# A block of gated experts, windowed attention and gated experts on one core: logits computed transposed, the gate products of the first and the last pass taken from PSUM, and a new order of the steps

## What is computed

```python
x = x + 0.5 * ffn(layernorm(x))
x = x + attn(layernorm(x))          # 16 heads, each token sees itself and the 63 before it
x = x + 0.5 * ffn(layernorm(x))     # the same weights as the first
```

```python
shared = silu(X @ sW1 + sb1) @ sW2 + sb2
logits = einsum('btd,ed->bte', X, routing_W) + expert_bias
top_vals, top_idx = top_k(sqrt(softplus(logits)), 2)
combine = sum(one_hot(top_idx, 8) * top_vals[..., None], axis=-2)
hdn = silu(einsum('nd,edh->enh', X, rW1) + rb1)
routed = einsum('ne,end->nd', combine, einsum('enh,ehd->end', hdn, rW2) + rb2)
```

## Time and profile before

| | |
|---|---|
| median of 3 runs | 1568.83 us (1565.42 to 1570.04) |
| the profiled execution | 1562.98 us, of it a span of 1561.1 us from the first to the last instruction |
| busy: PE, DVE, ACT, POOL | 97%, 76%, 72%, 51% |
| PE busy | 1506.6 us in 13969 matmul records |
| steps that mark the stages | aX0=0 at 74.95 us, O0=0 at 163.6 us, O0=1 at 259.6 us, O0=13 at 1351.3 us, S0=15 at 1428.03 us, O0=15 at 1502.93 us |

### The profile page before, as it was taken

One profiled execution on the slowest core, in us unless ns is written; L12 is line 12 of the kernel. 1 busy time (PEld: TensorE's weight loads), 2 busy tenths in 40 slices (PEclk: granted clock), 3 DMA queues, 4 the chain that ended last, 5 costly groups with the idle time before them and its releaser, 6 DMA issues.

```text
span 1561.1 us, 41431 instructions
## 1 busy us (share of the span) xinstructions
PE 1506.6 (97%) x13969; PEld 1359.6 (87%) x13969; DVE 1186.7 (76%) x4773; ACT 1127.8 (72%) x3416; POOL 790.8 (51%) x794
## 2 busy tenths in 40 slices
...
GB/s 118 15 203 103 148 120 186 106 137 133 119 170 96 188 119 131 136 125 168 104 187 112 137 130 135 157 119 177 109 138 141 119 159 108 174 108 155 84 28 14
DMA packets 264392, 199.66 MB, mean 128 GB/s; under 512 B 150859, under 2 KB 220918, under 8 KB 264182
## 3 DMA queue, kind: packets, MB, share of 16 engines
...
## 4 chain that ended last, share of the span: by engine, by line
PE 59%; DVE 15%; SPq 8%; issue 7%; ACT 5%; DMA 5%; POOL 2%; DVEq 0%; POOLq 0%; ACTq 0%
PE gb L1048 8%; PE gb L1050 8%; PE gb L1049 8%; PE yb L1048 6%; PE yb L1050 5%; PE yb L1049 5%; PE ptb L1121 4%; PE sb_ L1112 4%; SPq L570 4%; PE cxb L1140 3%; ACT pr L717 2%; SPq L565 2%; PE gb L1162 2%; DVE pr L920 1%; DVE ag L998 1%
## 5 line engine op out<-in xcount | busy, mean ns | idle before, releaser
L664 POOL TENSOR_TENSOR gl<-ag,gh 128x512 fp32r<-128x512 f32 x288 | 376.2, 1309 | 267.2 <-ACT gh L762 266.1
L647 POOL TENSOR_TENSOR pr<-pr,rinv 128x512 f32<-128x512 f32 x256 | 274.4, 1074 | 279.5 <-DVE rinv L928 276.6
L717 ACT ACTIVATE pr<-pr,mx 128x128 f32<-128x128 f32 x1024 | 396.4, 391 | 8.7 <-DVE mx L920 6.6
L1048 PE MATMUL yb<-w2h,gh 128*128 128x256 f32 x1152 | 334.7, 291 | 10.5 <-POOL gl L664 10.4
L1050 PE MATMUL yb<-w2l,gh 128*128 128x256 f32 x1152 | 321.7, 279 | 0.0
L1049 PE MATMUL yb<-w2h,gl 128*128 128x256 f32 x1152 | 321.6, 279 | 0.0
L775 ACT ACTIVATE tt<-gb,b1half 128x512 f32<-128x512 f32 x288 | 195.3, 680 | 130.1 <-PE gb L1050 125.9
L920 DVE CUSTOM_DVE_ANT_0 pr<-sb_,mask 128x128 f32<-128x128 f32 x1024 | 235.4, 285 | 36.8 <-issue 25.8
L992 DVE SCALAR_TENSOR_TENSOR ag<-gb,b,gate 128x512 f32<-128x512 f32 x256 | 190.0, 744 | 89.3 <-ACT tt L775 55.7
L1048 PE MATMUL gb<-xh,w1h 128*128 128x512 f32 x576 | 243.2, 422 | 1.7 <-DVE ag L992 1.3
L762 ACT ACTIVATE gh<-ag 128x512 fp32r<-128x512 f32 x288 | 179.9, 625 | 88.3 <-DVE ag L998 68.1
...
## 6 DMA issues: line engine op xcount, KB each, us to landing
...
ks<-qk_dram SPq DMA_DIRECT2D x256, 128.0 KB, 2.9
qs<-qk_dram SPq DMA_DIRECT2D x512, 64.0 KB, 2.5
...
```

Source lines behind the costliest of these rows:

```text
L647: nc.gpsimd.tensor_tensor(pr[:, k], pr[:, k], rinv[:, k, :].unsqueeze(2).to_broadcast([P, NP, P]), ALU.mult).then_inc(a_pn, 1)
L664: nc.gpsimd.tensor_tensor(gl[:, k, :], ag[:, k, :], gh[:, k, :].bitcast(F32), ALU.subtract).then_inc(f_gl, 1)
L717: nc.scalar.activation(pr[:, k, r, :], pr[:, k, r, :], ACT.Exp, bias=mx[:, k, r:r + 1], scale=-1.0, accum_out=rsum[:, k, r:r + 1]).then_in ...
L1048: nc.tensor.matmul(dst, ah, bh, start=start, stop=False, **kw)
```

## The change

It has five parts.

1. **Logits.** The routing weights (high and low half, padded with zeros to 128 columns) become the stationary operand, and the tokens stream past in 4 matmuls of 512 columns. A new ACT step `lt` copies the 128x512 result to the end of `xn`. A new PE step `M` multiplies each of its four 128x128 slices by a constant `fold` of 8 columns, which adds the halves and turns the logits back. `Lr` has one operation less.
2. **First and last pass.** Step `a` only adds the bias, and its result waits in a buffer that is free there (`kept`: halves of the residual buffers for experts 1 to 4, `gate` or `pt` for 5 to 8). `g` works in place. A new DVE step `m` multiplies it by the gate straight from `sb_` or `ptb` into `ag`. The eight ACT copies K of each of the two passes are gone, and with them their wait: H, t, a and g no longer need the gates.
3. **Buffers.** T of the second `ffn` writes to `axn`, and OUT reads it there. aR no longer waits for OUT; aN2 waits for the OUT of three samples before, T for the aX of two samples ahead. The last sample uses `xin` and the `p` half of `xh` and `xl`, so its start needs nothing of sample 14.
4. **Start.** Raw weights are staged in `gate`, `x2` and `axn`, and Wz waits for none of them any more. GpSimd has two more clears and two more selects.
5. **Order.** All of `HEAD`, `ORDER` and `TAIL` is new. Fillers fall from 159 to 88, all in `HEAD`.

```diff
-Z26=15 qX0=15 qX1=15 Z6=15 qL=15 qH0=15 Z30=15 qY0=15 qC=15 qH1=15 qH2=15 qH3=15 qB0=15 qB1=15 qB2=15 qB3=15
+S14=15 qY0=14 P12=15 S15=15 U11=15 P13=15 U13=15 P14=15 P15=15 qC=14 U15=15 O0=15 O1=15 qH1=14 qH2=14 qH3=14
...
-        rw = sb("rw", [P, KC, 2 * E], F32R)
+        rw = sb("rw", [P, KC, P], F32R)
+        fold = sb("fold", [P, E])
...
+        def kept(s, e):
+            if s[0] == "p" and e > 4:
+                return gate[:, e - 5, :]
+            if s[0] == "q" and e > 4:
+                return pt[:, e - 5, :]
+            two = (x1 if s[0] == "p" else [xin[(B - 2) % NXI], x1[(B - 2) % NX1]])[(e - 1) // 2]
+            u = 2 * ((e - 1) % 2)
+            return two[:, u:u + 2, :].rearrange("p t d -> p (t d)")
...
                 if s == "Wz":
                     nc.gpsimd.memset(qs[:].bitcast(F32), 0.0).then_inc(w_zero, 1)
-                    pool.wait_ge(w_lo, max(lo_done("1r"), lo_done("1t")))
                     nc.gpsimd.memset(va[:], 0.0).then_inc(w_zero, 1)
...
+                    wait(act, x_out, 16 * (b - 2))
...
+                elif s[1:] == "lt":
+                    n = nth(s, b)
+                    act.wait_ge(f_lgt, n + 1)
+                    nc.scalar.activation(lgt, bank(s[0] + "L", b), ACT.Copy).then_inc(f_lgs, 1)
...
-                elif s[1] == "K":
-                    n, m = nth(s, b), int(s[2])
-                    act.wait_ge(f_gpe, E * (s[0] == "q") + m + 1)
-                    wait(act, f_a, NE * (n - 1) + m + 6 if m < 4 else NE * n + m - 2)
-                    nc.scalar.activation(gate[:, m % 4, :], spread_to(m), ACT.Copy).then_inc(f_gk, 1)
...
-                op(nc.vector.tensor_tensor(lg[:], acc[:, :, E:2 * E], ebias[:].unsqueeze(1).to_broadcast([P, NT, E]),
-                                           ALU.add))
-                op(nc.vector.tensor_tensor(lg[:], acc[:, :, 0:E], lg[:], ALU.add))
+                op(nc.vector.tensor_tensor(lg[:], psum[:, 0:NT * E].rearrange("p (t e) -> p t e", t=NT),
+                                           ebias[:].unsqueeze(1).to_broadcast([P, NT, E]), ALU.add))
...
-                    wait(dve, x_out, 16 * b)
-                    nc.vector.tensor_tensor(x2[:, 2 * h:2 * h + 2, :],
+                    nc.vector.tensor_tensor(res(b)[:, 2 * h:2 * h + 2, :],
...
+                elif s[1] == "m":
+
+                    e = int(s[2])
+                    g = NE * nth(s, b) + e
+                    dve.wait_ge(f_gpe, E * (s[0] == "q") + e)
+                    dve.wait_ge(f_g, g + 1)
+                    wait(dve, f_gl, g + 1 - NG)
+                    nc.vector.tensor_tensor(ag[:, g % NG, :], kept(s, e), spread_to(e - 1), ALU.mult).then_inc(f_m, 1)
...
+                        rd, wr = res(b), axn
+                        dve.wait_ge(a_xt, min(2 * b + 6, 2 * B))
...
+                    for k in range(KC):
+                        nc.tensor.matmul(tile, rw[:, k, :], xh[:, q, k, :], start=(k == 0), stop=False)
+                        mm = nc.tensor.matmul(tile, rw[:, k, :], xl[:, q, k, :], start=False, stop=(k == KC - 1))
+                    mm.then_inc(f_lgt, 1)
+                elif s[1] == "M":
+                    n = nth(s, b)
+                    pe.wait_ge(f_lgs, n + 1)
                     for t in range(NT):
-                        ts = slice(t * P, (t + 1) * P)
-                        for k in range(KC):
-                            nc.tensor.matmul(tile[:, 2 * E * t:2 * E * t + 2 * E], xh[:, q, k, ts], rw[:, k, :],
-                                             start=(k == 0), stop=False, skip_group_check=True)
-                            mm = nc.tensor.matmul(tile[:, 2 * E * t:2 * E * t + E], xl[:, q, k, ts], rw[:, k, 0:E],
-                                                  start=False, stop=(k == KC - 1), skip_group_check=True)
+                        mm = nc.tensor.matmul(bank(s[0] + "L", b)[:, E * t:E * t + E], lgt[:, t * P:(t + 1) * P], fold[:],
+                                              start=True, stop=True, skip_group_check=True)
```

More of the change, by code:

```diff
@@ L21 @@
     "PE": """
[L22 to L26, removed]
+pY5-4 pH7-4 pH8-4 qH0-6 P5-5 pY6-4 S8-5 P6-5 U5-5 qC-6 S9-5 pY7-4 P7-5 S10-5 pY8-4 qH1-6 qH2-6 qY0-6 S11-5
@@ L30 @@
[L30 to L34, removed]
+qgh0-6 ph7-5 pN2-3 qt1-6 ex10-5 qt2-6 pxh0-3 cth0-5 qgh1-6 aN2-4 qgh2-6 qt3-6 qt4-6 pxh1-3 ph8-5 ex11-5
@@ L61 @@
[L61 to L69, removed]
+Z14=0 Wt=0 pX0=0 pX1=0 Z4=0 pL=0 pH0=0 pH1=0 pM=0 Z4=0 pH2=0 pH3=0 Z16=0 pY0=0 Z12=0 pC=0 pH4=0 pB0=0 pB1=0
+Z6=0 pB2=0 pB3=0 pH5=0 pH6=0 pH7=0 pY1=0 pH8=0 pY2=0 pB4=0 pB5=0 pX0=1 pY3=0 pX1=1 pY4=0 pB6=0 pB7=0 pY5=0
@@ new lines @@
+pxh0=3 aN2=2 qgh1=0 pxh1=3 qt3=0 qgh2=0 ex11=1 qt4=0 ph8=1 cth0=1 qgh3=0 axh0=2 axh1=2 qgh4=0 ph9=1 plt=3
+ex12=1 qt5=0 pen=3 qh00=2 ph10=1 qh01=2 ph11=1 qt6=0 ex13=1 qgh5=0 qt7=0 qt8=0 qgh6=0 qh10=2 ph12=1 ex14=1
+ph13=1 qgh7=0 pt0=3 ex15=1 qgh8=0 ph14=1 pcr=3 qh11=2 pct=3 pgh0=3 ph15=1 ex0=2 vh0=2 cth1=1 ex1=2 ex2=2
+vh1=2 ph0=2 ex3=2 pt1=3 pt2=3 ph1=2 qN2=1 pgh1=3 ph2=2 pt3=3 qxh0=1 pgh2=3 pt4=3 ex4=2 ph3=2 ex5=2 qxh1=1
+pgh3=3 pgh4=3 ex6=2 pt5=3 pt6=3 qlt=1 ph4=2 pgh5=3 qen=1 pgh6=3 pt7=3 pt8=3 ex7=2 ph5=2 qt0=1 pgh7=3 ph6=2
@@ new lines @@
+qH2=12 S11=13 pX0=15 qY0=12 pX1=15 P8=13 U7=13 qH3=12 S12=13 qH4=12 aX0=14 qY1=12 aX1=14 qY2=12 pL=15 P9=13
+qH5=12 pM=15 S13=13 Q00=14 P10=13 Q01=14 qY3=12 P11=13 qY4=12 P12=13 U9=13 U11=13 Q10=14 S14=13 Q11=14 pC=15
+S15=13 P13=13 qH6=12 qY5=12 P14=13 qH7=12 U13=13 P15=13 qH8=12 pH0=15 qY6=12 S0=14 U15=13 V0=14 qY7=12
+qY8=12 S1=14 P0=14 V1=14 pY0=15 pH1=15 O0=13 P1=14 O1=13 S2=14 pH2=15 pH3=15 S3=14 pY1=15 pH4=15 S4=14
+pH5=15 P2=14 qX0=13 S5=14 U1=14 P3=14 S6=14 pY2=15 qX1=13 pY3=15 pH6=15 pH7=15 qL=13 P4=14 pY4=15 qM=13
```

436 lines of the change are left out of this document (234 added, 202 removed).

## The result

The changed kernel takes 1606.66 us (median of 4 runs, 1598.16 to 1609.3) against 1567.12 us of the kernel before in the same session: ratio 1.0244, 95% interval 1.0198 to 1.029. It is slower by 2.4%; 1554 was forecast, and no rival named a cause like the one found. The profiled execution took 1607.88 us, its span 1606.2.

The account below looks back on a forecast made before the run. PE was taken to bound the kernel, busy 1506.6 of 1561.1 us, with waste at the ends. Terms -10 - 3 + 1 - 2 - 2 = -16 us, from 1568.8, gave 1554 us, range 1542 to 1571.

Parts of the forecast that it names:

- Ramp and middle: From 100 us through the middle samples: new order -2 us in the ramp, 0 in the middle, bounds -8 and +10.
- the tail: From S0=15 to the end: 58 + 65 = 123 us instead of 133.1, so -10 us, bounds -20 and -4.
- The second rival: End of kernel: attention of sample 15 stays at 70 us, partly at 1.2 GHz; no change, 1567 us; chance 0.14.
- Start: First stretch, bound by DVE: T=0 at 64.4 us, aX0=0 at 73; -2 us, bounds -5 and +3.
- the -3 of the moved V0, P14, U11 and U13: Four PE steps moved from before S0=15 to behind it; 3 us of PE work leave the full part.
- Ramp from S0 to O0=1: From 100 to 259.6 us: new order may save some idle time and half clock; -2 us, bounds -10 and +6.
- an attention of 70 us: Sample 15's attention stretch staying at 70 us instead of 58, tail 135 us, time 1567; also listed as a wrong sign.
- Logits: Each of 32 passes: four matmuls 0.92 us plus M 0.89 against 1.78 before; +1 us in all.
- The +29 us: Logits in 32 passes if each float32 pass had its own load, M costing 16 x 0.11; +29 us instead of +1.
- The first rival: Middle passes: M comes late, waiting for the ACT copy of the logits; 1 us a pass gives 1581; chance 0.12.
- What would show it: Signs: no filler behind 75 us, T=0 at about 64, tail 58 and 65 us, samples 91 us apart; also wrong signs.
- the mark of a wrong prediction: Middle samples: a round over 91.5 us, one of the listed signs that the forecast is wrong.

Follow-up runs that it names:

- the repaired kernel: Changed kernel with gates first on SP, S6 behind Y1, pN1 behind ri6, prs behind pn6, sp4 and sp5 ahead of ST10: 1551.14 us, ratio 0.9908.
- the kernel with H3 three times: Changed kernel with H3 of the p passes from sample 3 on computed three times into the same bank: 1596.87 us, ratio 1.0193.

## Why the prediction was wrong

**The step that failed** is "Ramp and middle ... **0**, bounds -8 and +10". It counted changes between kinds of step on PE and the waits of T, aN2 and aR, and never went through SP's list, although the change moved a transfer of 768 KB ahead of G1 there and although show a waiting for its gate in the kernel before (12.6 us). Nor did it follow DVE's list ahead of a1. The term is +61.7 us: 43.2 - 10.9 = 32.3 us of idle PE; 1110.2 - 1088.9 = 21.3 us of PE time that the repaired kernel, at clock 1.00, doesn't have; and 8.1 us by which PE is busier in the repaired kernel too (1088.9 against 1080.8). The 21.3 agree with the 21 us that the kernel with H3 three times gives. Of the 8 us, the distances of starts put most on P, the 128x128 transposes of attention: 79.7 us against 72.9 in the kernel before. In the new order 51 of its records of P stand behind a U, where 4 did, and the next start comes mostly 0.41 us or more behind them; of the old order's P most have it 0.36 behind. Why these neighbours cost more stays open.

**The rest of the sum held**, and the repairs show it: with all of them the kernel is 15.8 us faster by the medians of one session, where -16 was forecast. That this is so close is partly luck. By the two profiles it is 12.3 us, and the middle lost 7 us where 0 was forecast. In the changed kernel itself, the tail: -10 forecast, 133.1 - 120.8 = 12.3 measured; 58 us up to O0=15 were 53.8, 65 behind it were 67.0. ACT was 80% busy in the attention of sample 15, a little over my 75%, and its sum there was 43.2 us for the 43.7 reckoned. The second rival, a clock that eats the tail's gain, did not come: it was 0.90 there, and the stretch was short all the same. Start: T=0 at 62.95 instead of the forecast 64.4, aX0=0 at 70.8 instead of 73; -4.2 for -2, inside its bounds. From O0=13 to S0=15: 75.3 instead of 76.7, -1.4 for the -3 of the moved V0, P14, U11 and U13. Ramp from S0 to O0=1: 160.0 instead of 159.6, for -2. Three slips of arithmetic changed nothing: 1568.8 - 16 is 1552.8 and not 1554; an attention of 70 us gives 1565 by the prediction's own terms and not 1567; and V0, P14, U11 and U13 are taken off PE's work behind S0=15 in one place, where they were in fact added to it, as the next term says.

**Logits.** The price was right. L and M of sample 7 and their neighbours:

```profile
604.27 0.41 PE L1210 MATMUL gb<-xh,rw 128*128 128x512 f32 x1
604.51 0.39 PE L1211 MATMUL gb<-xl,rw 128*128 128x512 f32 x1
...
607.53 0.96 PE L1217 MATMUL gb<-fold,xn 128*128 128x8 f32 x8
608.34 0.47 PE L1099 MATMUL gb<-axh,wah 128*128 128x512 f32 x1
```

The four matmuls of L are 0.23 apart, M's eight records take 608.34 - 607.53 = 0.81 us where 0.89 was reckoned. The Trainium skill, "FP8 and Floating Point Precision", section "TensorE Precision Notes", has four passes for true float32. The +29 us that the prediction drew from it supposed that each pass is a record at 0.11 us; the trace excludes that, with eight records for M and not sixteen. It does not speak against four passes as such: a filler's record of 128 moving columns takes 0.115 us, and a reduced matmul of 512 columns 0.23, which is 0.06 for 128 by my estimate, so a filler's two records take the time of four such passes. With 8 moving columns that no longer shows. The first rival (M waits for the copy) didn't happen, since the cover was enough: PE waited 0.3 us for lt in the whole changed kernel. Without cover it costs 15 us.

**What would show it** was half right: no filler stood behind 75 us, T=0 and both halves of the tail came nearly as said, and the round was over 91.5 us, the mark of a wrong prediction: 93.3 to 98.4.
